# Second FFN weights: the first four loads and casts of the next output group put ahead of the group's epilogue

## The reference, cut to what matters

```python
xn = _layernorm(x)
x = x + attn(xn) + ffn(xn)          # attn: a gated state-space layer, 2048 inner channels

def ffn(x):                          # B*S tokens, DIM 1024, FFN 4096, E 8 experts
    route = softmax(x @ router_w + router_b)
    max_prob, max_ind = max(route), argmax(route)
    out = zeros_like(x)
    for e in range(8):
        a, g = split(x @ w1[e], 2)   # w1[e]: 1024 x 8192
        y = silu(a) * g @ w2[e]      # w2[e]: 4096 x 1024
        out = where(max_ind == e, y, out)
    return out * max_prob
```

## Time and profile before

| | us |
|---|---|
| median of 2 runs | 9373.39 (9350.86 to 9395.92) |
| the profiled execution, its own time | 8546.56 |
| its span on the slowest core (core 7) | 8544.9 |
| spans of the other cores | 8517.4 to 8542.8 |
| granted TensorE clock, mean of core 7 | 0.861 |

### The profile page before, as it was taken

How to read it: one execution, slowest core, us unless ns; L and a number is a source line. 1 busy time by engine, 2 the same in 40 slices (tenths; PEclk the granted TensorE clock), 3 DMA queues, 4 the chain that set the end, 5 groups by cost and what they waited for, 6 DMA issues and landing times.

```text
span 8544.9 us, 91984 instructions; the slowest of 8 cores (8517.4 to 8544.9 us)
## 1 busy us (share of the span) xinstructions
PE 6699.9 (78%) x29032; PEld 2889.9 (34%) x29032; DVE 3405.9 (40%) x6962; ACT 1681.0 (20%) x1615; POOL 135.3 (2%) x194
## 2 busy tenths in 40 slices
PE   3544548898998989899835445498989989899897
PEld 1211213343443434344312112143434434344343
DVE  4345443333343333433343454433343333433333
ACT  1211213031221302112112112131211213121120
POOL 1000000000000000000010000000000000000000
PEclk7657669999999999999966576699999999999998
DMA  2202113434443544434322021144343444444443
GB/s 80 70 30 72 57 40 131 124 140 138 130 146 127 152 126 140 142 124 153 118 94 70 30 74 55 40 138 129 138 139 127 154 132 141 136 133 146 129 151 114
DMA packets 418192, 963.06 MB, mean 113 GB/s; under 512 B 48608, under 2 KB 311040, under 8 KB 348096
## 3 DMA queue, kind: packets, MB, share of 16 engines
q1 hardware_dynamic: 410112, 939.71, 33.9%
q0 software_dynamic: 7616, 17.46, 0.6%
HBM read 948.33 MB, written 8.39 MB: 112 GB/s over the span
## 4 chain that ended last, share of the span: by engine, by line
PE 69%; DVE 15%; issue 6%; DMA 4%; ACT 4%; DVEq 1%; ACTq 1%; POOL 0%; SPq 0%; POOLq 0%
PE p_fo L1212 21%; PE p_fa L1127 20%; PE p_fg L1137 20%; PE p_z L409 2%; DVE tmp L353 2%; DVE acc L1259 2%; DVE tmp L1255 2%; PE p_w L922 2%; PE p_sb L633 2%; DMA stg<-wgate 1%; DMA stg<-w1t 1%; ACT L667 1%; ACT L362 1%; PE pY L795 1%; DMA stgw<-w2t 1%
## 5 line engine op out<-in xcount | busy, mean ns | idle before, releaser
L1212 PE MATMUL p_fo<-A,w2bf 128*128 128x512 bf16 x8192 | 1920.1, 400 | 422.3 <-DVE w2bf L1191 422.3
L1127 PE MATMUL p_fa<-xn,wbf 128*128 128x512 bf16 x8192 | 1855.5, 380 | 20.4 <-DVE wbf L1112 20.4
L1137 PE MATMUL p_fg<-xn,wbf 128*128 128x512 bf16 x8192 | 1851.6, 379 | 0.0
L1149 ACT ACT_TABLE_LOAD x512 | 656.9, 1283 | 4431.6 <-PE p_fa L1127 4431.6
L1082 DVE TENSOR_TENSOR A<-wbf,p_fg 128x1024 bf16<-128x1024 bf16 x512 | 625.3, 1221 | 2145.9 <-PE p_fg L1137 2145.1
L1212 PEld LDWEIGHTS p_fo<-A,w2bf 128*128 128x128 bf16 x8192 | 830.8, 102 | 1511.6 <-issue 642.3
L1127 PEld LDWEIGHTS p_fa<-xn,wbf 128*128 128x128 bf16 x8192 | 801.4, 98 | 993.2 <-issue 32.7
L1137 PEld LDWEIGHTS p_fg<-xn,wbf 128*128 128x128 bf16 x8192 | 801.5, 98 | 966.6
L1191 DVE CAST w2bf<-stgw 128x256 bf16<-128x256 f32 x2048 | 584.4, 293 | 1203.1 <-PE p_fo L1212 890.1
L1112 DVE CAST wbf<-stg 128x2048 bf16<-128x2048 f32 x484 | 593.8, 1227 | 49.4
L1149 ACT ACTIVATE wbf<-p_fa 128x1024 bf16<-128x1024 f32 x512 | 524.9, 1025 | 5.7
(11 more groups left out here) (145 smaller groups left out, 2643.2 us busy)
## 6 DMA issues: line engine op xcount, KB each, us to landing
stg<-w1t SPq DMA_DIRECT2D x512, 1024.0 KB, 4.9
stgw<-w2t SPq DMA_DIRECT2D x2048, 128.0 KB, 2.2
stg<-win_x SPq DMA_DIRECT2D x64, 512.0 KB, 3.5
stg<-wgate SPq DMA_DIRECT2D x64, 512.0 KB, 4.4
stg<-wout SPq DMA_DIRECT2D x32, 1024.0 KB, 5.8
stg<-win_b SPq DMA_DIRECT2D x64, 256.0 KB, 3.1
stg<-win_c SPq DMA_DIRECT2D x64, 256.0 KB, 3.0
acc<-u_t POOLq DMA_DIRECT2D x16, 512.0 KB, 10.0
```

The source lines that it names most:

```text
L1127: ins = t.matmul(p_fa[p][:, tsl * 512:(tsl + 1) * 512], wbf[:, p * 2048 + k * 128: p * 2048 + (k + 1) * 128], xn[:, k * HT + tsl * 512: k ...
L1137: ins = t.matmul(p_fg[p][:, tsl * 512:(tsl + 1) * 512], wbf[:, p * 2048 + 1024 + k * 128: p * 2048 + 1024 + (k + 1) * 128], xn[:, k * HT + ...
L1149: ins = s.activation(wbf[:, p * 2048: p * 2048 + 1024], p_fa[p][:, :], AF.Silu)
L1212: ins = t.matmul(p_fo[gp_par * 4 + o2 * 2 + tsl][:, :], w2bf[:, s4 * 256 + o2 * 128: s4 * 256 + (o2 + 1) * 128], A1[:, j * HT + tsl * 512: ...
```

## The change

The load and the cast of one step become a helper, `emit_w2_dc`, which takes the expert and the group to load for, the lists to record in and the two semaphore values to wait for. Behind the 32 steps of each group, and ahead of the `w1` prefetch and of the epilogue, the program now places the loads and casts of the first four steps of the *next* group: of `og + 1`, or of group 0 of the next expert behind group 3. Load `jn` waits for cast `28 + jn` of the present group, cast `jn` for its load and for the matmuls of step `28 + jn`. The next group takes the recorded values over and makes its own loads and casts from step 4 on. Behind group 3 of the last expert of a half nothing is placed, so group 0 of the first expert of a half makes its four itself, as before. The number of loads, casts and matmuls doesn't change, and the epilogue doesn't either.

```diff
+                    pend_w2 = state.get("w2_pend")
+                    state["w2_pend"] = None
                     for og in range(4):
                         gp_par = og % 2
-                        w2_dma, w2_cast, w2_mm = [], [], []
-                        for j in range(32):
+                        if og == 0 and pend_w2 is not None:
+                            w2_dma = list(pend_w2[0])
+                            w2_cast = list(pend_w2[1])
+                        elif og > 0 and state.get("w2_pend_next"):
+                            w2_dma = list(state["w2_pend_next"][0])
+                            w2_cast = list(state["w2_pend_next"][1])
+                            state["w2_pend_next"] = None
+                        else:
+                            w2_dma, w2_cast = [], []
+                        w2_mm = []
+
+                        def emit_w2_dc(j, tgt_e, tgt_og, dma_l, cast_l,
+                                       dma_guard, cast_guard):
                             s4 = j % 4
...
+                            def f_q(g, j=j, s4=s4, dg=dma_guard):
+                                if dg:
+                                    g.wait_ge(sems["ve"], dg)
                                 ins = g.dma_start(
                                     out=stgw2[:, s4 * 256:(s4 + 1) * 256],
-                                    in_=w2t[e, og, :, j * 256:(j + 1) * 256])
-                                w2_dma.append(inc(ins, f"dW{2 + s4}", 16))
+                                    in_=w2t[tgt_e, tgt_og, :,
+                                            j * 256:(j + 1) * 256])
+                                dma_l.append(inc(ins, f"dW{2 + s4}", 16))
                             sect("sync", f_q)
...
+                            def f_c(v, j=j, s4=s4, cg=cast_guard):
+                                v.wait_ge(sems[f"dW{2 + s4}"], dma_l[j])
+                                if cg:
+                                    v.wait_ge(sems["pe"], cg)
                                 ins = v.tensor_copy(
                                     w2bf[:, s4 * 256:(s4 + 1) * 256],
                                     stgw2[:, s4 * 256:(s4 + 1) * 256])
-                                w2_cast.append(inc(ins, "ve"))
+                                cast_l.append(inc(ins, "ve"))
                             sect("vector", f_c)
+
+                        for j in range(32):
+                            s4 = j % 4
+                            if j < len(w2_dma):
+                                pass
+                            elif j < 4:
+                                emit_w2_dc(j, e, og, w2_dma, w2_cast,
+                                           state["prev_w2_cast"],
+                                           state["prev_ffn_mm"] if og == 0 else None)
+                            else:
+                                emit_w2_dc(j, e, og, w2_dma, w2_cast,
+                                           w2_cast[j - 4], w2_mm[j - 4])
...
                         prev_cast = w2_cast
+                        nxt = None
+                        if og < 3:
+                            nxt = (e, og + 1)
+                        elif e < NE - 1:
+                            nxt = (e + 1, 0)
+                        if nxt is not None:
+                            n_dma, n_cast = [], []
+                            for jn in range(4):
+                                emit_w2_dc(jn, nxt[0], nxt[1], n_dma, n_cast,
+                                           w2_cast[28 + jn], w2_mm[28 + jn])
+                            if og < 3:
+                                state["w2_pend_next"] = (n_dma, n_cast)
+                            else:
+                                state["w2_pend"] = (n_dma, n_cast)
                         if og == 2 and e < NE - 1:
                             pf_dma, pf_cast = [], []
```

More of the change, by code:

```diff
@@ L1162, in ffn_phase @@
                     prev_cast = None
+                    pend_w2 = state.get("w2_pend")
+                    state["w2_pend"] = None
                     for og in range(4):
                         gp_par = og % 2
-                        w2_dma, w2_cast, w2_mm = [], [], []
-                        for j in range(32):
-                            s4 = j % 4
[L1169 to L1177, removed]
+                        if og == 0 and pend_w2 is not None:
[10 more added lines that the diff above has]
+                                       dma_guard, cast_guard):
+                            s4 = j % 4
+                            def f_q(g, j=j, s4=s4, dg=dma_guard):
+                                if dg:
+                                    g.wait_ge(sems["ve"], dg)
```

## The result

| | kernel before | changed kernel |
|---|---|---|
| median of all runs, us | 8939.81 (10 runs, 8538.38 to 9602.17) | 9135.70 (11 runs, 8367.37 to 9428.98) |
| fastest run, us | 8538.38 | 8367.37 |
| ratio of the comparable runs | 1 | 0.9778 (95% interval 0.9731 to 0.9825) |
| median core of a die that kept its full clock, mean over such dies, us | 8537.2 (25 dies) | 8357.1 (11 dies) |

A die's number here is the span of its median core, and a die counts when its mean clock is within 0.005 of the best of that kernel.

What follows compares the result with a forecast made beforehand. PE bounds the kernel, waiting 422.3 us for `w2` casts. Terms 111.2 + 29.6 + 28.1 + 17.6 + 0 − 8 = 178.5 us gave 8368 against 8546.6; the forecast took 190 us, 9183 us, range 9090 to 9305.

Steps and rivals of the forecast that it cites:

- the last one of the sum: Unexplained 827 us of the two runs shown: saving taken as 190 us, between 178 and that plus 24, giving 9183 us.
- its own bounds (68 to 283 us): Range of the whole saving, without the slower case and the outer ends; stated as 9090 to 9305 us.
- The wait moves four steps in and shrinks.: At 34 group boundaries of stage 2, PE's wait falls from 7.00 to 3.73 us, saving 111.2 us.
- Low clock after it.: Slower matmuls after those 34 waits cost 1.72 us each instead of 2.59, saving 29.6 us.
- Stage 1→2.: At 14 boundaries the 2.01 us wait ahead of group 0 goes: 28.1 us of waiting, 17.6 us of low clock.
- The `w1` prefetch.: At 14 boundaries between groups 2 and 3, `w1` lands four steps later, so the 10.83 us wait stays; saved: 0.
- Small costs.: Fourth casts waiting for loads cost 34 epilogues 5 us; later first work for the next stage 1 costs 3 us.
- The low clock did not stay: Rival: a 3.7 us wait costs as much clock as a 7 us one; saving 149 us, 9224 us, chance 0.12.
- the prefetch cost nothing at 2→3: Rival: `w2` loads hold up `w1`, the 2→3 wait grows to 14 us; saving 94 to 128 us, chance 0.12.
- the wait did not vanish: Rival: the wait at group boundaries vanishes or clock holds after short waits; saving 240 to 285 us, chance 0.06.
- The slower rival: With fewer gaps in dense matmuls the chip grants clock 0.81 for longer; 9540 us over all stage 2, chance 0.04.

Runs made afterwards that it cites:

- r8: The changed kernel with zeros passed for `w1` and `w2`, every instruction and transfer kept: all six runs 8366.33 to 8413.86 us.
- r4: The changed kernel with two steps made ready instead of four: 8412.7 us (3 dies).
- r5: The changed kernel with the epilogue of groups 0 to 2 cut into four pairs, placed between the next group's casts: 8152.3 us (7 dies).
- r1: The changed kernel with first steps made ready only for groups 1 to 3, not for group 0 of the next expert: 8404.3 us (6 dies).
- r2: The changed kernel with first steps made ready only for group 0 of the next expert: 8489.1 us (2 dies).
- r9: r5's split epilogue plus `w1` loaded in 64 KB pieces, every second step of groups 1 and 2, cast under groups 2 and 3: 8067.6 us (7 dies).

## Why the prediction was wrong, and where it was right

**The step that failed** is the last one of the sum: "The two runs shown are 827 us longer, and no row says why", and then 9183 us as if all runs to come were as long. The saving was measured as worked out (178.5 predicted, 180 and 171 measured), the ratio too (0.979 for 8368/8546.6, 0.9778 measured). The base was wrong. The cores of the two runs of 9350 and 9396 us are not on record, but in each of the 20 executions of the kernel before above 8600 us whose cores are, a die had lost clock. The eight further runs of this kernel were 8538 to 9602 us, four of them under 8580. And the profiled execution, with a clock of 0.99 in stage 1 on all eight cores, had told how long the kernel takes without that. The prediction should have given 8368 us, with the range 8264 to 8479 that its own bounds (68 to 283 us) make against the profiled execution.

That the median of all runs of the changed kernel, 9135.70 us, lies between 9090 and 9305 is luck and bears nothing out: the same median of the kernel before was 8939.81 us, so the medians move the other way, with how many executions lost clock.

The prediction even had the cause in hand. It priced a clock of 0.81 as a possible reason of the 827 us, and it cited the Trainium skill ("TensorE: Matmul & The Clock Gate", Part 1), by which dense matmuls on three or more cores take a die to 13/16 of its clock. It saw that the profiled execution disagreed and that by this rule the timed runs would be under it before and after, and it stopped there. The runs show something between. Dies at 0.81 there are, and with zero weights in r8 there are none of 12; that agrees with the same section of the Trainium skill, which says that all-zero operands don't trip it. The fixed outcome of the rule is not there: of the 172 dies in all executions with real weights whose cores are on record, 80 kept their full clock through the whole kernel.

**Right, point by point.**
*The wait moves four steps in and shrinks.* Predicted 3.73 us at 34 places, measured 3.65 at 31 and 4.8 at three. r4 and r5 show the chain.
*Low clock after it.* The interpolated 1.72 us gave groups of 29.51 us; the 28 unbroken groups average 29.47. That an average came out so is partly luck, for the price doesn't grow along a line: 16 of the 28 take 29.47 us, which is also what 12 of the 16 groups took after only 2 us of waiting, four take 27.8 us, and six take 30.3 to 30.6 us as after 7 us.
*Stage 1→2.* Predicted 28.1 + 17.6 = 46 us; r1 and r2 measure 46 and 48.
*The `w1` prefetch.* Predicted 10.83 us, unchanged; measured 10.97, and for the reason given. Against the end of the group the loads are issued 3.9 us later on average and the second cast comes 3.6 us later, where 3.47 were predicted. The wait list was to fall to 281 us and reads 286.8; in another execution a core of the undisturbed die has 281.7.
*Small costs.* Fourth casts that wait for their load were to cost 5 us; what the 34 waits hold above 3.58 us adds up to 5.7 us. Stage 1's waits were to grow by 3 us and grew by 4 to 5.

**The rivals.** The low clock did not stay (29.47 us and not 30.4), the prefetch cost nothing at 2→3 (10.97 us and not 14), and the wait did not vanish. The slower rival put the loss of clock down to fewer gaps. The change didn't bring it: 25 of 54 dies of the kernel before kept their full clock and 15 of 32 of the changed kernel (r9: 7 of 18). What such counts can't tell is a small shift.

## What to carry to other kernels

When the profiled execution and the runs shown differ by more than the change is worth, find out which of them is the kernel by itself before adding anything. A median of two is no base. Spans that agree across all eight cores are none by themselves either: in r2's profiled execution they lie within 9000 to 9055 us, and each die lost its clock for one half. The granted clock in a dense stretch tells, here 0.97 to 0.99 or 0.8. On an in-order engine, work made ready ahead of a long block takes its own length off the wait behind the block and no more; cutting the block up gave another 205 us on top of the 180. And the same bytes moved out of a wait can come back as late loads next to the stream that feeds the matmuls, so spread them: half as many pieces in a step gave back 51 us here.

## What the hardware showed that was not expected

A die's granted TensorE clock can fall to 0.81 for most of one FFN half and leave the other half alone, with 0.80 against 0.94 for the two dies in the same 900 us. In r2 this costs either die some 530 us (9028.5 and 9012.2 us against 8489.1). Other dies lost about twice that, 9554.7 against 8537.2 us, which would be both halves; this is an estimate, for no trace holds such an execution. Neither kernel is immune, and none of the edits changed how often it came in a way that the counts resolve. With zero weights it came in none of 12 dies. The price is large: 9396 us on the slowest core of one die in an execution whose other die took 8364. What decides whether a die loses its clock in an execution no run shows.
